# Another placement of the side work in a batched attention kernel: loop tables, order of the maxima, and the engine that spreads the keys

## The reference

```python
# 1: cross-attention, 16 heads of 64; context of 1601 tokens and the latents themselves are the keys
xn, l = layer_norm(ctx, g1, b1), layer_norm(layernorm(x), g2, b2)
q = l @ Wq
k, v = split(concat([xn, l]) @ Wkv)
x = x + (softmax(q k^T / 8) v) @ Wo
# 2: differential self-attention on the 64 latents, 16 heads, two maps of 8 features each, causal
A = softmax(Q1 K1^T / sqrt(8)) - lam * softmax(Q2 K2^T / sqrt(8))
O = A V;  O = O / sqrt(mean(O^2) + eps) * rms_scale * 0.2
x = x + O @ Wo.T                      # input: layernorm(x)
# 3: eight experts, the best two of them by a gate, weighted by a softmax
x = x + sum_e gate_e * (layernorm(x) @ expert_w[e] + expert_b[e])
```

## Time and profile before

| what | us |
|---|---|
| median of three runs | 955.99 |
| the three runs | 955.84, 955.99, 957.73 |
| the profiled execution | 953.88 |
| its span from the first to the last instruction | 952.1 |
| TensorE busy in the span | 914.6 |
| VectorE busy | 799.0 |
| ScalarE busy | 701.7 |
| GpSimd busy | 378.7 |

### The profile page before, as it was taken

The page is one execution under the profiler, slowest core; times in us unless marked ns, Lnnn a source line. Parts: engine busy times, 40 slices in busy tenths (PEclk is TensorE's granted clock), DMA queues, the critical chain, the costliest instruction groups (busy, mean ns, idle before and its releaser), DMA issues.

```text
span 952.1 us, 20497 instructions
## 1 busy us (share of the span) xinstructions
PE 914.6 (96%) x8246; PEld 491.8 (52%) x8246; DVE 799.0 (84%) x1591; ACT 701.7 (74%) x1003; POOL 378.7 (40%) x378
## 2 busy tenths in 40 slices
PE   8679999999999999999999999999999999999987
PEld 5444445555454545454545454545454545567653
DVE  5979898989797979797979797979797877598986
ACT  4767878787879796969797878787878677664633
POOL 6482134343434343334343434343434231354443
PEclk9889999999999999999999999999999999999987
DMA  6402030303040303030304030304030200000000
GB/s 213 83 12 61 11 84 8 88 6 90 1 94 2 95 1 95 1 95 2 94 1 94 1 95 1 91 5 88 7 73 11 45 15 24 1 24 24 2 2 22
DMA packets 74565, 41.95 MB, mean 44 GB/s; under 512 B 62276, under 2 KB 69864, under 8 KB 74472
## 3 DMA queue, kind: packets, MB, share of 16 engines
q1 hardware_dynamic: 74184, 39.60, 17.0%
q10 hardware_dynamic: 288, 1.05, 0.3%
HBM read 25.98 MB, written 0.59 MB: 28 GB/s over the span
## 4 chain that ended last, share of the span: by engine, by line
PE 81%; DVE 12%; ACT 3%; issue 2%; DMA 1%; POOL 0%; SPq 0%; DVEq 0%; ACTq 0%
PE S L2142 10%; PE S L2133 9%; PE OA L2166 9%; PE OA L2172 9%; PE OA L2169 9%; PE S L2136 9%; PE WW L2076 9%; PE S L1217 2%; PE WW L2063 1%; PE WW L2103 1%; PE WW L2104 1%; DVE amx L802 1%; PE WW L2105 1%; PE WW L2065 1%; PE WW L2064 1%
## 5 line engine op out<-in xcount | busy, mean ns | idle before, releaser
L1850 ACT ACTIVATE region<-S,sigma 128x1024 f16<-128x1024 f32 x208 | 231.7, 1114 | 135.1 <-PE S L2142 135.1
L1530 DVE TENSOR_TENSOR region<-S,region 128x1024 f16<-128x1024 f32 x208 | 252.3, 1213 | 42.5 <-ACT S L1854 42.5
L1518 DVE TENSOR_REDUCE mx<-WW 128x1 f32<-128x512 f32 (+1 forms) x480 | 262.6, 583 | 29.8 <-PE WW L2076 22.6
L1854 ACT ACTIVATE S<-S,sigma 128x1024 f32<-128x1024 f32 x208 | 224.5, 1079 | 0.0
L1662 POOL TENSOR_TENSOR xk<-raw,xk 128x508 f16<-128x508 f32 x64 | 63.3, 999 | 167.9 <-DVE xk L1397 167.9
L2076 PE MATMUL WW<-xT,region 128*128 128x512 f16 x360 | 124.8, 381 | 3.1 <-DVE region L1509 2.1
L2133 PE MATMUL S<-region,xT 128*128 128x512 f16 (+1 forms) x416 | 124.5, 380 | 3.3 <-DVE region L1530 2.6
L2166 PE MATMUL OA<-region,xk 128*128 128x512 f16 (+1 forms) x416 | 123.8, 379 | 0.0
L2136 PE MATMUL S<-region,xT 128*128 128x512 f16 (+1 forms) x416 | 123.7, 379 | 0.0
L2142 PE MATMUL S<-region,xT 128*128 128x512 f16 (+1 forms) x416 | 123.7, 379 | 0.0
L2172 PE MATMUL OA<-region,xk 128*128 128x512 f16 (+1 forms) x416 | 123.7, 379 | 0.0
(11 more groups left out here) (314 smaller groups left out, 1839.4 us busy)
## 6 DMA issues: line engine op xcount, KB each, us to landing
raw<-ctx SPq DMA_DIRECT2D x16, 768.0 KB
rb<-inv_dram SPq DMA_DIRECT2D x16, 512.0 KB, 3.6
xT<-xk SPq DMA_TRANSPOSE x48, 3.2
left_row<-left_pT SPq DMA_DIRECT2D x48, 2.0 KB
raw<-ctx SPq DMA_DIRECT2D x16, 32.5 KB
WO_lo<-L_xattn_Wq ACTq DMA_DIRECT2D x1, 512.0 KB, 3.8
WO_hi<-L_xattn_Wkv ACTq DMA_DIRECT2D x1, 512.0 KB, 4.6
lx<-x SPq DMA_DIRECT2D x1, 512.0 KB, 7.6
```

The lines of the kernel that those rows point to most:

```text
L1518: nc.vector.tensor_reduce(mx[:, r, c:c + 1], W[BANK[("m", n)]][:, 0:width], AX.X, ALU.max)\
L1530: nc.vector.tensor_tensor(p_lo[k], src, p_hi[k], ALU.subtract).then_inc(lo_done.sem, 1)
L1850: nc.scalar.activation(p_hi[k], src, ACT.Exp, scale=sigma[:, 0:1])
L1854: nc.scalar.activation(src, src, ACT.Exp, scale=sigma[:, 0:1]).then_inc(e_done.sem, 1)
```

## The change

All three tables get another order. `M_ORDER` becomes a mixed list of the same 32 pairs, and the waits for query parts and for the transpositions are put at the first maximum that needs each. ("q", 1) goes ahead of ("pj", 1); "left_turned" goes from unit 5 to unit 3 and "left" from unit 9 to unit 11; on VectorE the casts are spread over units 0 to 2, "combine" and "inverse" both stand in unit 4; the norms, the outputs' casts and the left-over key's items take other places on ScalarE. The early residual of the last slot starts in unit 4 instead of 3. In the self-attention the six calls of `keys` on VectorE are replaced by `spread_keys` on ScalarE, four activations with a column as the scale, behind the copy of the queries; the two calls in the last slot stay on VectorE.

```diff
--- before.py
+++ after.py
@@ -71,13 +71,20 @@
 
 
 
-LONG = [(r, c) for c in range(3) for r in range(8)]
-SHORT = [(r, 3) for r in range(8)]
-M_ORDER = LONG[0:6]
-for _k in range(8):
-    M_ORDER += LONG[2 * _k + 6:2 * _k + 8] + SHORT[_k:_k + 1]
-M_ORDER += LONG[22:24]
-assert sorted(M_ORDER) == sorted(LONG + SHORT)
+M_ORDER = [(0, 0), (4, 0), (3, 1), (5, 1), (0, 2), (3, 2), (3, 0), (1, 0),
+           (7, 1), (2, 1), (6, 0), (7, 0), (2, 0), (4, 3), (2, 2), (0, 3),
+           (7, 3), (4, 1), (1, 2), (5, 3), (0, 1), (5, 2), (1, 3), (6, 1),
+           (2, 3), (1, 1), (6, 2), (6, 3), (4, 2), (3, 3), (5, 0), (7, 2)]
+assert sorted(M_ORDER) == [(r, c) for r in range(8) for c in range(4)]
+
+
+def first_of(test):
+    return [test(r, c) for r, c in M_ORDER].index(True)
+
+
+Q_FIRST = {first_of(lambda r, c: r // 4 == k): k for k in range(2)}
+Q_LATENTS = {first_of(lambda r, c: c == 3 and r // 4 == k): 2 + k for k in range(2)}
+XT_FIRST, XT_SECOND = first_of(lambda r, c: c < 2), first_of(lambda r, c: c >= 2)
 
 
 def some(first, count):
@@ -87,47 +94,47 @@
 
 
 TENSOR = [([], [("weigh", 12)]),
-        ([("left_scores", 0), ("q", 0), ("pj", 0)], []),
-        ([("pj", 1), ("q", 1)], some(0, 1)),
-        (some(1, 1), some(2, 2)),
-        (some(4, 1), some(5, 1)),
-        ([("left_turned", 0), ("q", 2), ("q", 3)], some(6, 1)),
+        ([("left_scores", 0)], [("q", 0), ("pj", 0)]),
+        ([("q", 1), ("pj", 1)], some(0, 1)),
+        (some(1, 1), some(2, 1) + [("left_turned", 0)]),
+        (some(3, 2), some(5, 1)),
+        ([("q", 2), ("q", 3)], some(6, 1)),
         (some(7, 2), some(9, 2)),
         (some(11, 2), some(13, 1)),
-        (some(14, 2), some(16, 2)),
-        (some(18, 2), some(20, 1) + [("left", 0)] + some(21, 2)),
+        (some(14, 2), some(16, 3)),
+        (some(19, 2), some(21, 2)),
         (some(23, 2), some(25, 2)),
-        (some(27, 2), some(29, 3)),
+        (some(27, 2), some(29, 1) + [("left", 0)] + some(30, 2)),
         ([("mt", 0), ("mt", 1)], [("weigh", 11)])]
 
-VECTOR = [("stat", "stat", "stat", "stat", "latents", "stat", "left_sum", "low", ("split", 0), ("split", 1), "stat", ("q", 0), ("split", 2), "stat",),
+VECTOR = [("stat", "stat", "stat", "stat", "latents", "stat", ("split", 0), "left_sum", "low", ("split", 1), ("q", 0),),
+          (("split", 2), "low", "stat",),
+          ("stat", "stat", "stat", "low", ("split", 3), ("q", 1), "stat", ("m", 0), ("m", 1), "left_low", "stat", "stat", "stat", ("m", 2),),
           ("low",),
-          ("stat", "stat", "low", "stat", "left_low", ("split", 3), ("q", 1), ("m", 0), ("m", 1), "stat", ("m", 2), "stat", ("m", 3), "stat",),
-          ("low", ("m", 4), ("m", 5),),
-          ("combine", "low", ("q", 2), ("q", 3), ("m", 6),),
-          ("low", ("m", 7), ("m", 8), "inverse", ("m", 9), ("m", 10),),
-          ("low", ("m", 11), ("m", 12), ("m", 13),),
+          (("m", 3), ("m", 4), "combine", ("m", 5), "low", "inverse", ("q", 2), ("q", 3), ("m", 6),),
           ("low",),
-          (("m", 14), ("m", 15), ("m", 16), ("m", 17), "low", ("m", 18), ("m", 19), ("m", 20), ("m", 21), ("m", 22),),
+          (("m", 7), ("m", 8), ("m", 9), ("m", 10), "low", ("m", 11), ("m", 12), ("m", 13),),
+          ("low", ("m", 14),),
+          (("m", 15), ("m", 16), ("m", 17), ("m", 18), "low", ("m", 19), ("m", 20), ("m", 21), ("m", 22),),
           ("low",),
           (("m", 23), ("m", 24), ("m", 25), ("m", 26), "low", ("m", 27), ("m", 28), ("m", 29), ("m", 30), ("m", 31),),
           ("low",),
           ("low",)]
 
 SCALAR = [([], [], ["outputs"]),
-          ([], [], [("q", 0)]),
-          ([], [], ["projected", "left_exp", ("q", 1)]),
           ([], [], []),
+          ([("q", 0), "left_exp"], [("q", 1)], ["projected"]),
+          ([], [], ["left_copy"]),
           ([], [], []),
-          (["left_copy"], [("q", 2), ("q", 3)], []),
-          ([], [("norm", 0)], []),
-          ([("norm", 1)], [], [("norm", 2)]),
-          ([], [("norm", 3)], [("norm", 4)]),
-          ([("high", 0)], [("norm", 5)], []),
-          ([], [("norm", 6)], [("norm", 7)]),
-          ([("high", 1)], [("norm", 8), ("norm", 9)], [("norm", 10)]),
-          ([("norm", 11), ("norm", 12)], [], [("shift", 0), ("shift", 1)])]
-LEFT_AT = 9
+          ([], [("q", 2), ("q", 3)], []),
+          ([("norm", 0)], [], []),
+          ([], [], []),
+          ([("norm", 1), ("norm", 2)], [], [("high", 0)]),
+          ([], [], [("norm", 3), ("norm", 4), ("norm", 5), ("norm", 6)]),
+          ([("norm", 7)], [], [("norm", 8), ("norm", 9)]),
+          ([], [("high", 1)], []),
+          ([("norm", 10), ("norm", 11), ("norm", 12)], [("shift", 0)], [("shift", 1)])]
+LEFT_AT = 11
 
 
 def bank_of_items():
@@ -589,7 +596,7 @@
         LAST_OUT = {("pj", k): OA[:, 1, :] for k in range(2)}
 
         EARLY = TB - 1
-        X1_AT, H_AT, TILE0_AT, KEYS1_AT, VALUES1_AT = 3, 8, 9, 10, 11
+        X1_AT, H_AT, TILE0_AT, KEYS1_AT, VALUES1_AT = 4, 8, 9, 10, 11
 
         PJ_SIDE, X1_SIDE, H_SIDE, SIDES = 2, 3, 4, TB + 1
         GATES = (range(0, 5), range(5, TB))
@@ -794,6 +801,16 @@
             k_ = src.rearrange("p (c n) -> p c n", c=2).unsqueeze(2).to_broadcast([128, 2, 4, 128])
             p_ = pick[:].unsqueeze(1).to_broadcast([128, 2, 4]).unsqueeze(3).to_broadcast([128, 2, 4, 128])
             nc.vector.tensor_tensor(Kx[t.off % 2][:], k_, p_, ALU.mult).then_inc(ta["kx"].sem, 1)
+
+        def spread_keys(act, t):
+            wait(act, "projqk", t)
+            if t.off >= 2:
+                act.wait_ge(ta["scores"].sem, ta["scores"].upto(t.plus(-2), 1))
+            for k in range(4):
+                ins = nc.scalar.activation(Kx[t.off % 2][:, :, k, :],
+                                           W[0][:, 256:512].rearrange("p (c n) -> p c n", c=2), ACT.Copy,
+                                           scale=pick[:, k:k + 1])
+            ins.then_inc(ta["kx"].sem, 1)
 
         def tail_vector(dve, link):
             def maxima(t, k):
@@ -922,8 +939,6 @@
                     side_reads(m - 1)
                 if m + 1 < TB:
                     maxima(t.plus(1), 0)
-                if m + 2 < TB:
-                    keys(dve, t.plus(2), W[0][:, 256:512])
                 if m == TB - 1:
                     first0, second0 = gating(0)
                     first0()
@@ -1073,6 +1088,7 @@
                     projected(LAST)
                 if m + 2 < TB:
                     queries(act, t.plus(2), W[0][:, 0:256])
+                    spread_keys(act, t.plus(2))
                 if 0 < m < TB - 1:
                     values(act, t.plus(1), W[1])
                 weights(t, 0)
@@ -2065,11 +2081,13 @@
                         ins = mm(dst, G_lo[:, h, c:c + 128], cT_hi[p][:], start=False, stop=True)
                 if kind == "m":
                     r, c = M_ORDER[k]
-                    if r % 4 == 0 and c in (0, 3):
-                        pe.wait_ge(q_hi_done.sem, q_hi_done.upto(turn, r // 4 + (2 if c == 3 else 0)))
-                    if (r, c) == (0, 0):
+                    if k in Q_FIRST:
+                        pe.wait_ge(q_hi_done.sem, q_hi_done.upto(turn, Q_FIRST[k]))
+                    if k in Q_LATENTS:
+                        pe.wait_ge(q_hi_done.sem, q_hi_done.upto(turn, Q_LATENTS[k]))
+                    if k == XT_FIRST:
                         pe.wait_ge(xt_first.sem, landed(turn))
-                    if (r, c) in ((0, 2), (0, 3)):
+                    if k == XT_SECOND:
                         pe.wait_ge(xt_second.sem, landed(turn))
                     rows = q_hi[p][:, 128 * r:128 * r + 128]
                     if c < 3:
@@ -2086,8 +2104,6 @@
                                  start=True, stop=True)
                 if kind == "left_turned":
                     pe.wait_ge(left_low.sem, left_low.upto(turn))
-                    if turn is LAST:
-                        pe.wait_ge(x1_read.sem, 1)
                     ins = mm(w[:, 0:128], left_p[:], ident16[:], start=True, stop=True)
                 if kind == "mt":
                     pe.wait_ge(m16_done.sem, m16_done.upto(turn))
@@ -2216,9 +2232,9 @@
                         pe.wait_ge(free["pj"].sem, free["pj"].upto(Turn(2 * EARLY - 1)))
                         pe.wait_ge(free["ol"].sem, free["ol"].upto(LAST.plus(-1), 1))
                         pe.wait_ge(free["left_scores"].sem, free["left_scores"].upto(LAST))
+                        pe.wait_ge(free["left_turned"].sem, free["left_turned"].upto(LAST))
                         early_x1(pe)
                     if b is LAST and u == H_AT:
-                        pe.wait_ge(free["left_turned"].sem, free["left_turned"].upto(LAST))
                         early_columns(pe)
                     if b is LAST and u == TILE0_AT:
                         wait(pe, "hcopy", Turn(0))
```

## The result

The changed kernel takes 970.9 us (median of six, 969.0 to 976.9) against 955.8 us for the kernel before it: a ratio of 1.0186, 95% interval 1.0154 to 1.0217, which is 15 to 21 us slower. The two medians by themselves stand 15.0 us apart, a quotient of 1.0157; how the recorded ratio is formed from the same executions is not on record. I had forecast 960.0 (951 to 966): the direction is right, the size is not. In the file after the change most lines stand 16 further on: the scores are L2149 to L2158, the maxima L2094 to L2097, `left_turned` L2107, `left_low` L1555; the last slot's tiles are L668 and their transposes L649.

What follows compares the result with a forecast made beforehand. Tensor work was taken to bound the loop. Slots with a load +5.2, slots 13 and 14 -0.4, slot 0 -0.5, last slot +1.0, keys -1.5: +3.8 on 955.99 gives 959.8, said as 960 us, range 951 to 966.

Steps and rivals of the forecast that it cites:

- four tiles take 1.1 [...] three tiles 0.8: Last slot, VectorE: time to normalise the early residual's seven tiles, ending at 809.9, so TensorE waits 1.0 us.
- the third cast's 1.40: VectorE, unit 1: 1.40 us beside GpSimd's subtraction, should fall to 0.4 in the new order; counted as nothing.
- The maxima: TensorE's holes in units 3, 10 and 11 close, saving 0.67 us a slot; new hole of 0.35 at maximum 18.
- The reciprocals: Moved to unit 4, they wait for `rcol` to land: 0.65 us at maximum 6, 0.1 at maximum 10, twelve slots.
- my terms for them: Slots 1 to 14: +5.2 us for the twelve with a context load, -0.4 for slots 13 and 14.
- The residual's 1.0: Last slot: early residual starts one unit later, so TensorE waits at its transposes, +1.0 us (ends 0 and 2).
- The norms and `outputs_high` that move on ScalarE stay in its free time: ScalarE, busy 38.5 of 47.9 us a slot: the moved items count nothing, 0.3 a slot as the bad end.
- The keys: Self-attention: six VectorE multiplications become four ScalarE copies per iteration at 0.36 a step, -1.5 us (ends -4 and +3).
- Dearer wait: Rival: `rcol` lands 5.2 us after issue as a rule, 1.8 a slot, +19 us, 975; chance 0.05.
- holes where I see none, in unit 3: Sign of being wrong: holes in unit 3, second remainder's margin being 0.06, make each slot longer still; no size given.

Runs made afterwards that it cites:

- experiment 1: Changed kernel with `left_low` put ahead of `low_part` in unit 2, where GpSimd stands still: 1.0099 of the kernel before.
- 2: Changed kernel with VectorE's order untouched, GpSimd's sum of the denominators made to wait for `left_low`: 1.0128 of the kernel before.
- 10: Kernel before with `left_low` alone moved behind maximum 1 in unit 2, beside GpSimd's sum; `left_turned` stays in unit 5: 1.0126 of the kernel before.
- 3: Changed kernel; in the last slot GpSimd's scaling of the outputs waits until VectorE has normalised the seven tiles: 1.0144 of the kernel before.
- 12: Changed kernel with `left_low` ahead of `low_part` and, in the last slot, GpSimd's scaling behind VectorE's seven tiles: 1.0067 of the kernel before.
- experiment 6: Changed kernel with `left_low` ahead of `low_part` in unit 2 and the reciprocals back behind maximum 8: 0.9969 of the kernel before.
- experiment 5: Changed kernel with only the reciprocals (`"inverse"`) put back behind maximum 8: 1.0165 of the kernel before.
- 9: Kernel of experiment 6 with ScalarE's first `outputs_high` back from the end of unit 8 to the head of unit 9: 0.9997 of the kernel before.
- 11: Kernel of experiment 6 with the self-attention's key multiplications back on VectorE: 1.0007 of the kernel before.

## Why the prediction was wrong

**The step that failed** is in the part by part costing: `left_low` and `left_turned` move and my text puts no price on either, and of the last slot's tiles it says "four tiles take 1.1 [...] three tiles 0.8". Both take the durations of the trace before for operations that the new order sets beside GpSimd. `left_low` goes from 0.14 to 1.70 us, and TensorE starts 1.29 late behind it fourteen times (15.8 us in the list of waits); four tiles take 4.96 instead of 1.1, and TensorE waits 5.3. The first is shown by experiments 1, 2 and 10, the second by 3, and 12 shows that with both gone 6.4 us remain, where my sum has 3.8. The means were in my own text: it explains the third cast's 1.40 by GpSimd's subtraction beside it. I used that for the operation that left such a place and did not ask which ones entered one.

**The maxima.** Right: three holes gone, a new one of 0.33 for 0.35. But 0.67 less 0.35 was worth 0.12 a slot net, not 0.32 (experiment 6), because of small holes that I had not seen: 0.13 at the start of a slot, up to 0.2 at maximum 29.

**The reciprocals.** The mechanism was right, the size near. In experiment 1 maximum 6 starts 0.88 us late on average in the twelve slots with a load, where I had 0.65 (median 0.66 over slots 1 to 13). In the list of waits these are 12 of the 14, with 8.6 of the 10.3 us; the other two, 0.85 each, stand in slots 0 and 1, and in experiments 5 and 6 too. In the changed kernel four of the twelve are left, with 1.5 of the 3.2 us listed, because TensorE is already 1.29 late there. The two waits overlap and do not add. Slot 13 waits as well, by 0.16: SP's list there has a load that I overlooked, 512 KB of `x` straight ahead of `rcol`. Already in the kernel before, `rcol` landed 3.75 us behind its issue there:

```profile
702.00 0.58 SPq L1346 DMA_DIRECT2D raw<-x  x1
702.63 0.58 SPq L512 DMA_DIRECT2D rcol<-srow  x1
```

**Luck in the loop.** With the first collision gone (experiment 1) slots 1 to 14 take 5.2 us more than before, and my terms for them add up to +4.8. Yet neither part came out: the maxima brought 1.7 us (experiment 6) where I had 4.5, and the reciprocals cost 7.0 (experiment 1 less 6) where I had 9.2. The two errors cancel.

**The last slot.** The residual's 1.0 was 0.8. Beside the collision I missed a second queue: "The norms and `outputs_high` that move on ScalarE stay in its free time" is true of the loop and false in the last slot, where the cast stands ahead of the copies of the transposed tiles (1.75 us of TensorE in experiment 6, gone in 9; 1.1 in experiments 3 and 12).

**The keys.** -0.4 to -0.9 for -1.5, and four copies at a step of 0.36 as I took it (the profile shows 0.48 for each).

**The rivals.** "Dearer wait" had nearly the right size (975; with its other terms, which it leaves out, 973.6) for a wrong reason: the transfer landed as before (3.6 to 5.4 us behind its issue with a load, median 3.9). The signs that would prove me wrong named "holes where I see none, in unit 3", which is where it is, but with the second remainder as the cause.

**A version that beats the kernel before** I did not get with certainty: experiment 6 is 0.3% faster than before by its timed runs, its trace accounts for 0.2 us of that, and its two neighbours 9 and 11 are at 1.000. At equal clock experiments 6 and 9 are 1.1 and 1.2 us faster, experiment 11 is level. Why the clock of the same kernel differs from one execution to the next stays open.

## What to carry to other kernels

When work is moved on VectorE, list what GpSimd does at the new time, not only whether VectorE is free: an operation of eight columns that reads two SBUF tensors costs what GpSimd's running instruction has left. A duration from the trace belongs to the operation and its neighbours. And when several waits follow each other in one loop, price the one that comes first: the later ones may be hidden by it, and undoing them, as experiment 5 did, tells nothing until it is gone.

## What the runs showed of the hardware

- VectorE is held up per instruction of GpSimd. Beside back-to-back scalings of 1.25 us it got through one tile for each, 1.30 us apiece (0.34 alone).
- Not drawn out beside GpSimd: maxima out of PSUM (0.68 with and without), `low_part` with one PSUM and one SBUF input (1.215 in both), the statistics of one SBUF tensor (0.277 in both), and the scaling of 128x8 with one SBUF input ahead of the reciprocals (0.161 in both). So it is not the small size that is hit.
- The self-attention ran at a granted clock of 0.91 to 0.98 from run to run, with no edit to go with it, and took 4 to 5 us more at 0.92 to 0.93 than at 0.97 to 0.98. Spans of single profiled runs of this kernel should be compared by stretches of equal clock.
